# Where five engines are told of a branch: the hint at the head of the first pass or a few steps from its end

## What is computed

```
x = x + L0_attn(xn) + L0_ffn(xn)      # causal, 32 heads of 8; FFN in fp8, gelu
xn = layernorm(x)
x = x + L1_attn(xn) + L1_ffn(xn)      # mixes the 16 heads of one row; ternary weights, silu, rms norm
```

## Time and profile before

| | us |
|---|---|
| median of 3 runs | 603.89 |
| lowest and highest | 603.83, 605.21 |
| the profiled execution | 603.83 |
| its span, first to last instruction | 602.1 |

### The profile page before, as it was taken

The page is one execution under the profiler, slowest core; times in us unless marked ns, Lnnn a source line. Parts: engine busy times, 40 slices in busy tenths (PEclk is TensorE's granted clock), DMA queues, the critical chain, the costliest instruction groups (busy, mean ns, idle before and its releaser), DMA issues.

```text
span 602.1 us, 13153 instructions
## 1 busy us (share of the span) xinstructions
PE 560.9 (93%) x5035; PEld 290.9 (48%) x5085; DVE 444.4 (74%) x905; ACT 467.7 (78%) x605; POOL 257.8 (43%) x318
## 2 busy tenths in 40 slices
PE   4687898999999999999989999999999999999997
PEld 2332433444455455554535555555444454356665
DVE  6899998879787764785987868648454646467967
ACT  2499899987779988899668787887889797874451
POOL 4773966145626335233765638225052240261200
PEclk9699999999999999999999999999999999999999
DMA  8630110030430233001104032340410501334542
GB/s 285 248 106 2 36 36 1 1 53 3 70 53 11 47 44 53 1 2 29 19 0 73 0 54 49 51 53 10 80 20 2 88 1 29 51 54 80 106 62 56
DMA packets 150912, 30.38 MB, mean 50 GB/s; under 512 B 133952, under 2 KB 149568, under 8 KB 150848
## 3 DMA queue, kind: packets, MB, share of 16 engines
q1 hardware_dynamic: 150272, 29.19, 24.5%
q10 hardware_dynamic: 576, 0.33, 0.3%
HBM read 19.02 MB, written 10.49 MB: 49 GB/s over the span
## 4 chain that ended last, share of the span: by engine, by line
PE 65%; DVE 16%; ACT 8%; issue 6%; DMA 3%; POOL 1%; SPq 1%; DVEq 0%; ACTq 0%
PE psV L693 16%; PE psS L679 7%; ACT Pt L934 4%; PE psA L842 3%; PE psS L796 3%; PE psA L861 2%; PE psB L842 2%; PE psC L842 2%; DVE ga L1296 1%; DMA stage<-in_wg 1%; PE psA L758 1%; PE psC L861 1%; PE psB L861 1%; PE psC L730 1%; DVE ga L1293 1%
## 5 line engine op out<-in xcount | busy, mean ns | idle before, releaser
L934 ACT ACTIVATE Pt<-psS 128x1024 f32<-128x1024 f32 x288 | 280.1, 1031 | 54.1 <-PE psS L679 29.6
L693 PE MATMUL psV<-Pt,vaug 128*32 128x512 f32 x1152 | 146.5, 602 | 3.7 <-DVE ob L1256 1.5
L1591 POOL TENSOR_SCALAR_AFFINE_SELECT Pt<-Pt 128x1024 f32<-128x1024 f32 x64 | 74.7, 1191 | 52.9 <-ACT Pt L934 52.6
L679 PE MATMUL psS<-qTf,kTf 32*128 32x512 f16 x576 | 72.5, 387 | 3.1 <-ACT Pt L934 1.5
L679 PEld LDWEIGHTS psS<-qTf,kTf 32*128 32x128 f16 x576 | 19.2, 91 | 75.5 <-ACT Pt L934 37.7
L693 PEld LDWEIGHTS psV<-Pt,vaug 128*32 128x32 f32 x1152 | 26.1, 108 | 50.1 <-issue 36.1
L1646 POOL TENSOR_TENSOR ss<-ss,mhalf 128x1 f32<-128x1 f32 x16 | 9.0, 564 | 92.0 <-DVE ss L1425 91.9
L983 ACT ACTIVATE stage<-psS 128x1024 f32<-128x1024 f32 x32 | 31.0, 1022 | 7.9 <-PE psS L796 7.5
L1637 POOL TENSOR_TENSOR r<-qk,cos 128x256 f32<-128x256 f32 x16 | 14.2, 888 | 47.4 <-ACT qk L967 47.4
L1582 POOL TENSOR_TENSOR QXf<-rt,QXf 128x512 f16<-128x512 f32 x16 | 19.5, 1216 | 26.1 <-ACT QXf L921 26.1
L1620 POOL TENSOR_SCALAR rs<-mv 128x1 f32<-128x1 f32 x16 | 4.5, 283 | 52.4 <-DVE mv L1319 52.3
(11 more groups left out here) (375 smaller groups left out, 1290.9 us busy)
## 6 DMA issues: line engine op xcount, KB each, us to landing
qkvscr<-rqkv SPq DMA_DIRECT2D x16, 384.0 KB, 2.6
G<-qkvscr SPq DMA_DIRECT2D x24, 128.0 KB, 3.8
stage<-in_wg SPq DMA_DIRECT2D x4, 512.0 KB, 7.8
oscr<-o SPq DMA_DIRECT2D x16, 128.0 KB, 3.0
w8g<-qkvscr SPq DMA_DIRECT2D x16, 128.0 KB, 3.7
at<-oscr SPq DMA_DIRECT2D x16, 128.0 KB, 2.2
out<-yout SPq DMA_DIRECT2D x16, 128.0 KB, 2.7
x<-in_x SPq DMA_DIRECT2D x1, 1536.0 KB, 12.0
```

Source lines behind the costliest of these rows:

```text
L679: e.matmul(psS[j], kd[32 * j:32 * j + k, h, 128 * at:128 * at + 128], qd[32 * j:32 * j + k, 4 * h:4 * h + 4, :].rearrange("p s n -> p (s n ...
L693: ins = e.matmul(psV[32 * j:32 * j + 32, :], vaug[:, at, j, 32 * h:32 * h + 32], Pt[(4 * Q + j) % NP], start=(kb == 0 and h == 0), stop=(k ...
L934: e.activation(flat(Pt4[:, u % NP:u % NP + 2, :]), flat(psS4[:, j:j + 2, :]), ACT.Exp, scale=scale).then_inc(S["exp"], 1)
L1591: e.affine_select(out=p, in_=p, pattern=[[0, 8], [1, 128]], compare_op=ALU.is_ge, fill=0.0, base=0, channel_multiplier=-1).then_inc(S["mas ...
```

## The change

The hint moves, on every engine, to a place a few steps before the end of the first pass: 3 steps on SP, 8 on PE and DVE, 2 on ACT and POOL. No step changes, and none changes its place among the others.

```diff
@@ sp
             load_rest()
+            steps = first_pass("sp")
+            for name, n in steps[:-3]:
+                run[name](n)
             ahead = e.mark_branch_hint_location()
-            for name, n in first_pass("sp"):
+            for name, n in steps[-3:]:
                 run[name](n)
@@ pe
+            steps = first_pass("pe")
+            for name, n in steps[:-8]:
+                run[name](n)
             ahead = e.mark_branch_hint_location()
-            for name, n in first_pass("pe"):
+            for name, n in steps[-8:]:
                 run[name](n)
...
```

More of the change, by code:

```diff
@@ L1007, in act @@
             load_small()
+            steps = first_pass("act")
+            for name, n in steps[:-2]:
+                run[name](n)
             ahead = e.mark_branch_hint_location()
-            for name, n in first_pass("act"):
+            for name, n in steps[-2:]:
                 run[name](n)
@@ L1502, in dve @@
                    "ssm": ssm, "hx": hx, "hTc": hTc, "at1Tc": at1Tc, "yo": yo, "yout": yout}
+            steps = first_pass("dve")
+            for name, n in steps[:-8]:
+                run[name](n)
             ahead = e.mark_branch_hint_location()
-            for name, n in first_pass("dve"):
+            for name, n in steps[-8:]:
                 run[name](n)
@@ L1649, in pool @@
                    "ge4": ge4, "xf": xf, "rs1": rs1, "xl": xl, "ro1p": ro1p, "rsg": rsg}
+            steps = first_pass("pool")
+            for name, n in steps[:-2]:
+                run[name](n)
             ahead = e.mark_branch_hint_location()
-            for name, n in first_pass("pool"):
+            for name, n in steps[-2:]:
                 run[name](n)
```

## The result

| | us |
|---|---|
| changed kernel, median of 6 runs | 607.55 (606.81 to 608.12) |
| kernel before, median of 6 runs | 604.15 (603.83 to 605.21) |
| ratio | 1.0054, 95% interval 1.0041 to 1.0067 |
| profiled execution, and its span | 608.02, 606.3 |

The change costs 3.4 us. The likeliest case, no change, did not come; the first rival did in kind, but it was priced at 2.0 us, and the time lies above the range.

A forecast was written before the change was run, and what follows sets the result against it. The chain lies mostly on PE (65%), untouched; only the uncovered branches at the end could matter. All terms were 0: 603.83 + 0 = 603.8, but added to the median 603.89, giving 603.9 us; range 603.0 to 607.0, 8 in 10.

The forecast's parts named there:

- The likeliest case: At the branches, late hints are acted on at once, so branches cost what they did: 0 us, 603.9, chance 0.54.
- the first rival: Behind the branch on PE and SP: the late hint comes too late, +2.0 us, 605.9 (604.9 to 608.1), chance 0.36.
- What bounds the kernel, and where the change can act: Chain mostly on PE (65%); the change acts only at hints and branch, where 2.2 us of sequencer work has no cover.
- Whether the target was there before: At the branches: target lines had already arrived, at least three of four engines holding theirs 70 us before branching.
- The hint's own time and the shift by one slot: At old and new hint places and in code lines: 50 to 55 ns per hint, covered; both terms taken as 0.
- a late hint is acted on at once: Between hint and branch: the sequencer fetches the target within the 6 to 9 us available, adding 0 us.
- The price of a miss: Behind the branch: the target is fetched after branching, +1.0 to +4.2 us, taken as +2.0.
- a second wait: On PE behind the branch: possibly waiting also for the line behind the target, another 2.6 us.
- the hint had never mattered: Rival at the branch: the target would be there for another reason, no change, 603.9, chance 0.06.
- a pending hint costs something at each line change: Rival at the 64 line changes, 40 on PE: 0.1 us cheaper each on PE, 599.9, chance 0.04.
- The tests I had named: Between 592 and 600: code packets per late hint and drains 0.4 to 0.5 us behind branches, or no packets and later drains.
- my sign of being wrong altogether: At the flag: written at another time than 599.7 by more than the spread of runs.

The follow-up runs named there:

- e1: Kernel before with no branch hint on any engine: 608.40 us against 604.77, ratio 1.0045 to 1.0087.
- e5: Kernel before with SP's hint alone moved, to 3 steps before the end: 607.47 us against 604.48, ratio 1.0036 to 1.0075.
- e3: Kernel before with hints of SP, ACT, POOL and DVE moved ahead of each engine's last code line change: 604.61 us against 604.77.
- e4: Kernel before with hints of SP, ACT, POOL and DVE moved behind each engine's last code line change: 607.22 us against 604.77.
- e7: Kernel before with PE's hint alone moved, to 27 steps before the end: 605.28 us (one run).
- e2: Kernel before with PE's hint alone moved, to 8 steps before the end: 604.69 us against 604.77, ratio 0.9992 to 1.0014.
- e9: Kernel before with PE's hint alone moved, to 6 steps before the end: 605.55 us (one run).
- e10: Kernel before with PE's hint alone moved, to 7 steps before the end: 603.83 us (one run).
- e6: Kernel before with PE's hint alone moved, to 1 step before the end: 607.58 us (one run).

## Why the prediction was wrong, point by point

**What bounds the kernel, and where the change can act.** Right. +3.1 of the profiled 4.2 us lie between flag and end. That the branch has only sequencers beside it, and no cover, was right.

**Whether the target was there before.** Right: e1 shows the alternative, with drains 2.9 to 4.0 us behind the branches. The Trainium skill, "Runtime: NRT & Kernel Launch", section "Instruction fetch mechanics", says that a taken branch outside the window stalls for its page; with no hint, and with one that comes too late, the traces agree (3.9 us on PE in e1, 3.6 on SP in e5). My reading of the mechanism, that the target takes the next line's place when the branch's line is entered, is borne out for four engines: the place by e3 and e4, the replacing by the equal counts of packets with and without hints. On PE it fits e7: 41 packets, none out of turn. My own ground for it, that slots fetched and executed agree, was weaker than I wrote: of the 13,440 slots 512 came behind the branches, which leaves 12,928 for 13,153 instructions. The rest must have come ahead of the span, where I did not count, so a line fetched in vain could not have been seen that way.

**The hint's own time and the shift by one slot.** Nothing seen of either: e2, e3, e7, e9 and e10 end 2.35 to 2.36 us behind the flag, and all but e2 reach it 7.97 us behind the read.

**The step that failed: that a late hint is acted on at once.** I gave that 0.54 and the opposite 0.36, on the ground that the hints at the head were silent because the branch was far. The rows could not decide between them. The answer was yes on PE and no on the other four, which my cases did not allow for: I treated the five sequencers as one kind. Since the slowest engine sets the barrier, one "no" was enough, as e5 shows, and so the chance of a miss somewhere was larger than for any one engine. That follows from the barrier's rows, and I could have counted it.

**The price of a miss.** I added 1.1 us to the packet's start and 0.5 us for its length, called that a lower bound, and took +2.0. The first two terms were right for SP, ACT, POOL and DVE (0.9 to 1.0 us and 0.3 to 0.5 us). The mis-sized term is the one that I left without a row, from the packet's end to the first instruction: it measured 2.0 to 2.5 us on these four in the changed kernel (1.4 to 1.8 in e1, without hints), and 2.2 in e5, where SP's packet starts at 602.36 and takes 0.48 us and its drain is at 605.1. With it the price is +3.1 us to the span, inside the bounds of 1.0 to 4.2 that I had; but I took a value in their lower half and cut the range at 607.0 instead of carrying the upper bound through to 608.1. That the bounds held it is luck: the 4.2 came from a second wait, for the line behind the target, on PE. No run has that wait (in e1 PE's drain is at 605.2 and the next 16 KB packet at 605.9), and in the changed kernel PE did not miss at all.

**The other rivals.** That the hint had never mattered falls with e1 (+3.6 us). That a pending hint costs something at each line change has nothing for it: with PE's hint held from 0.9 us or from 575.6 (e7), all else is alike, and e2 and e3 are not faster than before.

**Collision.** I set the fetch of a served hint beside the work at no cost. In the changed kernel and e2 it met the last read of `oscr` and cost 0.64 and 0.83 us up to the flag. Taken together, 3.1 + 0.6 = 3.7 us against 3.4 in the medians, whose interval is 2.5 to 4.0.

**The tests I had named** worked: I said that packets between 592 and 600 would mean a served hint and their absence a late one. PE had its packet, the other four had none. The work up to the flag was not the same, as I had asked of the first rival. The flag came at 600.81 instead of 599.73; 1.1 us is within the spread of the first runs before (603.83 to 605.21), so my sign of being wrong altogether did not appear, though 0.64 us of it are the collision and not spread.

## What to carry to other kernels

A prefetch hint for a branch belongs well ahead of it: on these engines ahead of the change of code line before the branch. The head of the straight-line code satisfies this where, as here, the code is longer than one line; a place "a few steps before" does not. Behind a barrier it is the worst engine that counts, so judge an edit made on five engines by the chance that any one fails. And when a price has a term that no row shows, carry its upper bound into the range.

## What the runs showed of the hardware that I had not expected

- A taken branch whose target is not at hand took 2.9 to 4.0 us to the next instruction, of which the transfer of the line is only 0.3 to 0.5 us on ACT, POOL, DVE and SP (1.0 to 1.1 on PE, in e1 and e6). With the target there it took 0.45 to 0.62 us.
- On those four engines the miss was longer with a late hint (3.2 to 4.0 us in the changed kernel, e4 and e5) than with none (2.9 to 3.3 us in e1). The difference lies behind the packet: 2.0 to 2.5 us from its end to the drain in all nine late cases, 1.4 to 1.8 in the four of e1. So on these engines a late hint looks worse than none. PE shows no such difference (1.4 us in both e6 and e1), and since it misses too in e1, at 4.0 us, e1 ends only 0.14 us earlier. No run takes away the hint of one of the four alone, which would show what a late hint itself costs.
- PE acts on a hint inside the branch's line, with 1.1 to 4.2 us delay; SP, ACT, POOL and DVE did not in up to 230 us.
- One 16 KB packet of code made the last read of `oscr` (128 KB) land 1.7 to 1.9 us later when it started 1.1 to 1.3 us behind its issue (changed kernel, e2), and not at all when it started 1.6 us behind (e10). The read near 375 us has the same edge, between 1.55 and 1.56 us.
